# Another order of the steps of four engines between the long convolution and the second feed-forward block, with unread products ahead of 17 waits of TensorE

## What is computed

```
K  = 2 Re(sum over 64 modes of Ct exp(dtA l))           a convolution kernel for each of 256 channels
y  = irfft(rfft(x) * rfft(K)) + D x                     a convolution along 1024 tokens
x1 = layernorm(x + (layernorm(x + y) * w + b))
x2 = layernorm(x1 + attention(x1, ctx) Wo + bo)         16 heads of 16, 77 keys
s  = top 8 of (8 best row keys + 8 best column keys), for each of 4 heads
e  = sum over heads and k of silu(x2 . down[idx]) softmax(s) up[idx]
out = layernorm(x2 + (silu(x2 Wg + bg) (x2 Wu + bu)) Wd + bd + e)
```

## Time and profile before

| | |
|---|---|
| median of 3 runs | 652.65 us (652.47 to 652.74) |
| the profiled execution | 650.57 us |
| its span, first to last instruction | 648.8 us |
| TensorE busy / weight loads | 587.8 us (91%) / 383.0 us |
| VectorE busy | 493.2 us (76%) |
| ScalarE busy | 397.8 us (61%) |
| GpSimd busy | 310.8 us (48%) |
| mean granted clock of TensorE | 0.961 |

### The profile page before, as it was taken

The page is one execution under the profiler, slowest core; times in us unless marked ns, Lnnn a source line. Parts: engine busy times, 40 slices in busy tenths (PEclk is TensorE's granted clock), DMA queues, the critical chain, the costliest instruction groups (busy, mean ns, idle before and its releaser), DMA issues.

```text
span 648.8 us, 9695 instructions
## 1 busy us (share of the span) xinstructions
PE 587.8 (91%) x3186; PEld 383.0 (59%) x3186; DVE 493.2 (76%) x966; ACT 397.8 (61%) x554; POOL 310.8 (48%) x346
## 2 busy tenths in 40 slices
PE   5569799988976899999999999999999999998996
PEld 2246576766645554547867455785755587543585
DVE  7999985565688779977677897677688886778872
ACT  4777573304344579777638887754788754777750
POOL 0737586684334564333555423356443262744441
PEclk9679999979977899999999999999999999999998
DMA  8591327782700000000000000000000000000000
GB/s 240 196 367 72 107 75 199 174 165 23 317 0 1 2 2 1 0 1 2 1 8 9 10 9 0 2 0 10 9 9 9 1 2 1 17 9 8 1 17 17
DMA packets 19819, 33.88 MB, mean 52 GB/s; under 512 B 7248, under 2 KB 14161, under 8 KB 18321
## 3 DMA queue, kind: packets, MB, share of 16 engines
q1 hardware_dynamic: 15393, 29.06, 14.4%
q10 hardware_dynamic: 4376, 4.20, 2.3%
HBM read 21.55 MB, written 10.26 MB: 49 GB/s over the span
## 4 chain that ended last, share of the span: by engine, by line
PE 65%; DVE 19%; ACT 6%; POOL 3%; issue 3%; DMA 2%; DVEq 0%; POOLq 0%; SPq 0%; ACTq 0%
PE banks L838 22%; PE banks L930 8%; PE banks L935 8%; PE banks L885 4%; PE banks L907 3%; PE banks L862 3%; PE banks L897 3%; DVE stats L1481 2%; PE banks L871 2%; PE banks L922 2%; PE banks L711 2%; DVE arena L1445 2%; DVE arena L1569 1%; PE banks L768 1%; DMA arena<-scr_x 1%
## 5 line engine op out<-in xcount | busy, mean ns | idle before, releaser
L1277 POOL TENSOR_TENSOR arena<-arena 128x1024 f32<-128x1024 f32 x64 | 126.3, 1973 | 155.8 <-ACT arena L1150 154.7
L838 PE MATMUL banks<-arena 128*128 128x512 f32 x384 | 174.2, 596 | 5.7 <-issue 3.6
L838 PEld LDWEIGHTS banks<-arena 128*128 128x128 f32 x384 | 69.9, 190 | 83.1 <-issue 77.2
L1150 ACT ACTIVATE arena<-arena 128x1024 f32<-128x1024 f32 x64 | 73.5, 1149 | 7.5 <-DVE arena L1567 3.2
L1152 ACT ACTIVATE arena<-arena 128x1024 f32<-128x1024 f32 x64 | 73.5, 1149 | 2.1
L1569 DVE SCALAR_TENSOR_TENSOR arena<-arena 128x1024 f32<-128x1024 f32 x48 | 65.1, 1357 | 1.7
L1248 POOL TENSOR_SCALAR arena<-mv 128x1 f32<-128x1 f32 (+1 forms) x40 | 14.4, 361 | 100.6 <-DVE mv L1482 99.2
L930 PE MATMUL banks<-arena 128*128 128x256 f32 x256 | 58.4, 381 | 2.7 <-DVE arena L1591 1.3
L1040 ACT COPY arena<-banks 128x512 f32<-128x512 f32 (+1 forms) x64 | 34.1, 533 | 43.3 <-PE banks L830 31.2
L935 PE MATMUL banks<-arena 128*128 128x256 f32 x256 | 57.9, 379 | 0.0
L1054 ACT ACTIVATE tok<-tok,arena,rstd 128x256 f32<-128x256 f32 x48 | 27.9, 598 | 45.8 <-POOL arena L1253 44.9
(11 more groups left out here) (183 smaller groups left out, 1076.7 us busy)
## 6 DMA issues: line engine op xcount, KB each, us to landing
scr_x<-arena SPq DMA_DIRECT2D x16, 256.0 KB, 2.5
arena<-scr_x SPq DMA_DIRECT2D x2, 2048.0 KB, 11.2
scr_z<-arena ACTq DMA_DIRECT2D x13, 256.0 KB, 3.9
tok<-in_x SPq DMA_DIRECT2D x8, 256.0 KB, 5.3
arena<-scr_z SPq DMA_DIRECT2D x4, 512.0 KB
out<-tok SPq DMA_DIRECT2D x16, 128.0 KB, 1.7
arena<-scr_z SPq DMA_DIRECT2D x2, 640.0 KB
arena<-in_imat SPq DMA_DIRECT2D x1, 1152.0 KB, 5.3
```

The lines of the kernel that those rows point to most:

```text
L838: ins = mm(bk[:, :], w[:, k, P * m:P * m + P], src[:, k, :], start=(k == 0), stop=(k == KC - 1))
L1150: fn(ebuf[m % 2], sxb[m % 2], ACT.Prelu, bias=negt[:, n % 2, h:h + 1], alpha=FAR).then_inc(s_ranked, 1)
L1277: tt(sxb[m % 2], sim[:, n % 2, h, 0:XR].unsqueeze(2).broadcast_to((P, XR, NKEYS)), sim[:, n % 2, FH + h, :].unsqueeze(1).broadcast_to((P, ...
```

## The change

Three things. A table `MOVED` gives, for each engine, a new place in time to some steps; all others keep theirs. Counted as the fewest steps that have to be taken out and put elsewhere, 50 of TensorE's steps change their place, 72 of ScalarE's, 47 of VectorE's and 23 of GpSimd's, all ahead of inner.1.0 on TensorE (tile 10); behind it the lists are the same. The three groups of unread products become 17, each at the head of a step and ahead of its waits (apart from those for its bank): 38 products in place of 11, with the sixteen behind the convolution kept. And `rconv` of the last two steps lies elsewhere in the arena.

The diff, cut to its core:

```diff
+MOVED = {
+    "pe": {('conv', 7): -1.14, ('score', 0, 0): -0.75, ('score', 1, 0): -0.18, ('probs', 1, 0): 0.81,
...
+        ('score', 5, 0): 4.18, ('sim', 1): 4.2, ('score', 5, 1): 4.22, ('expert', 0, 3): 4.42,
...
+    "act": {('norm1', 0): -1.32, ('conv', 7): -0.06, ('score', 1, 1): 0.65, ('probs', 1, 0): 0.7342,
...
+    "dve": {('ln', 2): -1.14, ('ln', 3): -1.02, ('ln', 4): -0.89, ('residual', 2): -0.76, ('ln', 5): -0.46,
...
+    "pool": {('values', 0): -0.8, ('dev0', 2): -0.96, ('dev1', 2): 2.3, ('dev1', 3): 2.46, ('dev2', 0): 2.63,
...
-WARM = ((-0.5, 4, ("probs", 0, 0)), (-0.1, 5, ("probs", 0, 0)), (0.6, 2, ("turno", 0)))
+WARM = {('turn1', 0, 0): 1, ('turn1', 0, 1): 5, ('query', 0, 0): 1, ('score', 0, 0): 1, ('score', 0, 1): 1,
+        ('score', 1, 0): 3, ('probs', 1, 0): 4, ('score', 2, 1): 3, ('project', 1): 1, ('score', 3, 1): 5,
+        ('turno', 2): 5, ('probs', 3, 0): 1, ('project', 3): 1, ('sim', 0): 1, ('expert', 0, 0): 1,
+        ('probs', 4, 0): 1, ('probs', 4, 2): 3}
...
-    for at, count, before in WARM:
-        steps.append((at, ("warm", count, before)))
...
-    return [y for _, y in sorted(steps, key=lambda v: v[0] + LAG.get((engine, v[1][0]), 0.0))]
+    moved = MOVED[engine]
+    return [y for _, y in sorted(steps, key=lambda v: moved.get(v[1], v[0] + LAG.get((engine, v[1][0]), 0.0)))]
...
-        rconv = part("rconv", o_w + 4096, TILES, D)
+        rconv_of = [part(f"rconv{h}", at, B, D) for h, at in enumerate(
+            [o_w + 4096 + B * D * q for q in range(NQ - 2)] + [o_ext, o_ext + B * D])]
...
-            def warm(count, bk):
+            def idle(count, columns, start=True):
 
                 for _ in range(count):
-                    mm(bk[:, 0:D], ident[:, :], wq[:, 0, :], start=True, stop=True)
+                    mm(columns, ident[:, :], wq[:, 0, 0:columns.shape[-1]], start=start, stop=True,
+                       skip_group_check=True)
+
+            def idle_turn(step):
+
+                if step in WARM:
+                    later = PLAN[PLAN.index(step):]
+                    idle(WARM[step], t_unit(next(y for y in later if y in T_AT))[:, 0:D])
+
+            def idle_wide(step):
+
+                if step in WARM:
+                    idle(WARM[step], w_unit(step + ("a",))[:, 0:D])
...
                 elif kind == "probs":
                     j = step[2]
+                    idle_turn(step)
                     pe.wait_ge(s_exp, 2 * n + 2)
...
                 elif kind == "project":
+                    idle(WARM.get(step, 0), bank[4][:, 0:D])
                     pe.wait_ge(s_tev, T_AT[("turno", n)] + 1)
```

More of the change, by code:

```diff
@@ L818, in conv @@
                         conv_half(ahead, 0)
-                    warm(WARM_CONV, bank[4])
+                    idle(WARM_CONV, bank[4][:, 0:D])
                     pe.wait_ge(s_zr[1], 16 * (len(z_batches()) - 2 + 3))
@@ L880, in _ @@
                         if c % 4 == 0:
+                            idle(WARM.get(step + (c // 4,), 0), bank[4][:, 2 * P + 16:4 * P], start=False)
                             pe.wait_ge(s_tev, T_AT[("probs", n, c // 4)] + 1)
```

56 lines of the change are left out of this document (51 added, 5 removed), and 3 rows, old and new, of the table MOVED.

## The result

The changed kernel takes 658.22 us, the median of 8 executions (656.57 to 661.27), the kernel before in the same session 652.69 (8 executions, 650.44 to 658.34). The ratio is 1.0078, with a 95% interval of 1.005 to 1.0106: **0.8% slower, where 1.1% faster was forecast**. The profiled execution of the changed kernel took 660.39 us (span 658.6), that of before 650.57 (span 648.8).

The account below looks back on a forecast made before the run. VectorE was taken as the bound ahead of expert.0.0, TensorE behind it. 11.0 - 5.15 + 1.7 - 0.5 = 7.05, so 7 us less: 645.6 us from 652.65, range 640.8 to 649.8.

Parts of the forecast that it names:

- 11.0 us of lead: Up to expert.0.0: shorter waits on VectorE's chain let it start at 218.55 in place of 229.54.
- the cover of the five products ahead of score.3.1: Ahead of score.3.1 on TensorE: five unread products, 2.3 us, fit in a wait of 2.6 and cost nothing.
- the 0.5 us put against the moves whose lengths were not followed: Tiles 5 to 9: new waits among the other moved steps cost 0.5 us, bounds none and 1.7 us.
- the first score's wait: VectorE ahead of score.0.0: its idle 8.91 us shrink to a wait of 0.65 us.
- probs.4.2: Behind 218.5: TensorE waits 0.95 us for its bank, then three products take 1.35, together 2.3 us.
- The clock, 1.00 throughout: TensorE ahead of expert.0.0: 87% busy, against 85% in a stretch that kept 1.00, so full clock throughout.
- Given back behind 218.5, 5.15 us: Where TensorE is the bound: new waits at probs.4.0, score.5.1 and probs.4.2 cost 5.15 us together.
- The wait at score.5.1: Behind sim.1: TensorE waits 2.0 us while best.0 takes 5.8; were best.0 some 3.8, no wait, 9 us gained.
- probs.4.0: Behind 218.5: TensorE waits 0.85 us for the exponential of score.4.1, its one product inside that wait.
- The two gaps that close, 1.7 us: TensorE's gaps at turno.4 (0.76 us) and expert.1.0 (0.94) close, 1.7 us gained.
- Rival 4: Unread products stand uncovered on the path, deciding at some 60% uncovered: 4.7 us more, 657 us; chance 0.05.
- All three signs: expert.0.0 later than 223, clock below 0.9 between 186 and 218, or TensorE gaps over 2 us between tiles 5 and 9.

Follow-up runs that it names:

- The ladder: The medians of the kernels that ran, in rows that mostly differ by one named change; together some 9 us of gain and 15 us of loss.
- the kernel with the free bank: The changed kernel with the five products ahead of score.3.1 written to unread columns of bank 4 instead of a transpose bank: 652.46 us, ratio 1.0003.
- the mended kernel: Kernel before plus early moves (to expert.0.0) and their products, those at score.3.1 in free bank-4 columns, norm1.7 moved to 4.09: 643.44 us, ratio 0.986.
- the mended kernel with the moves from place 7.9 on: The mended kernel with the late moves of place 7.9 and later (tiles 8 and 9) added, norm1.7 excepted: 646.96 us, ratio 0.9918.
- the pair of runs with and without the products: The mended kernel, 643.44 us, and the same with `WARM = {}` (convolution's sixteen products kept), 652.03 us.
- The late part: The moved steps with places from 3.95 on (tiles 4 to 9); put alone into the kernel before, with its products: 665.11 us, ratio 1.0182.
- the order without products: The changed kernel with none of its 38 unread products, the sixteen behind the convolution kept: 660.33 us, ratio 1.0107.
- the early part alone: Only the moves ahead of the first feed-forward block, with all products but the three at probs.4.2, later steps as before: 652.47 us, ratio 1.0002.
- the kernel without that group: The changed kernel without the five unread products ahead of score.3.1, nothing else: 655.23 us, ratio 1.0042.

## Why the prediction was wrong, step by step

Forecast were 11.0 us of lead, 3.95 us given back behind it (5.15 - 1.7 + 0.5) and nothing for the products: 7 us less. The ladder has 9.1 us of lead, 9.0 given back and 5.8 for one group of products: 5.7 us more, beside 5.5 measured. Two terms failed. One is the cover of the five products ahead of score.3.1, costed at nothing; the other is the 0.5 us put against the moves whose lengths were not followed.

**The lead, 11.0 us: nearly right as a walk, wrong in one cover.** The parts that I followed came as written: the first score's wait (1.05 us after 8.91; I had said 0.65), and in the kernel with the free bank expert.0.0 62.0 us after turn1.0.0 where I had 60.1, so a lead of 9.0 us. (The walk was short by the other 2 us: project.3 came at 215.40 in the mended kernel, where I had 213.3.) The step that failed is "five before score.3.1 (2.3 in 2.6)", costed at nothing. I asked how long TensorE would wait for the score's own semaphore and whether the products fit in. I did not ask what the **products** wait for, though the change puts each group ahead of its step's waits "apart from those for its bank". For probs.4.2, which waits in the same way for a bank, I did see it. The wait for the bank ends at 200.30, 1.4 us after the wait it was to fill (198.88), and costs 5.8 us of the kernel, as the run with the free bank shows.

**The clock, 1.00 throughout: right but for that place.** It was 1.00 up to 186 us, 0.89 to 218, and 1.00 there too once the five products ran in time. One trace speaks against a full cure: in the mended kernel with the moves from place 7.9 on, TensorE's list and its waits from turn1.0.0 to 198 us are those of the mended kernel, but the five products of turno.2 took 4.09 us for 2.40 and the clock from 186 to 218 was 0.95.

```profile
198.43 4.09 PE L811 MATMUL banks<-wqo,ident 128*128 128x256 f32 x10
```

The Trainium skill, TensorE: Matmul & The Clock Gate, "What's actually happening", has the throttled state as the default that activity releases; the pair of runs with and without the products (1.00 and 0.80) agrees. My weighing of 87% busy against 85% was no argument for it: in the changed kernel the stretch from 186 to 229.5 is 84% busy and has 0.92, because of the one piece of it that ran at half the clock behind one idle time.

**Given back behind 218.5, 5.15 us: some 3.1 us of it came.** The wait at score.5.1 was to be 2.0 us and was 0.36, because best.0 took 4.3 us and not 5.8 (229.16 to 233.46; this was the other end that I had kept). At probs.4.2 I had 0.95 and 1.35: it was 1.03 and 1.56. At probs.4.0 I had 0.85: it was 0.19.

**The two gaps that close, 1.7 us: they did not.** turno.4 waits 0.69 us where it waited 0.76, and sim.4 with expert.1.0 together 1.11 where it was 0.49 and 0.94.

**"0.5 against it for the moves of tiles 5 to 9": the worst-sized term.** The late part costs 9.0 us by the ladder, where 5.15 - 1.7 + 0.5 made it 3.95. With 3.1 us for the waits that I followed and nothing for the gaps, some 6 us are left for this term, where I had 0.5. What I had not followed is in it: the waits at sim.2 of 1.17 us, at 284.41 of 0.65, at 286.12 of 0.44, at 366.33 of 0.62, and the 2.8 us behind inner.1.0. My bounds for it were "none, and the 1.7 us themselves": I took it that these moves could lose no more than they might win, and no row said so. Moved steps whose lengths are not followed need a bound from the trace on both sides; TensorE was busy 113.1 of 115.5 us there, so they could win 2.4 us at most in that stretch, and what they could lose had no such bound.

**Rival 4, slower at 657 us, chance 0.05,** gave nearly the right time for half of the reason; that its number came so close is luck. It named the products on the path, with 60% of them uncovered as the point where it decides. One group of 17 was on the path, and by its bank. The other half, the late part, stood in no rival. All three signs that I had named for "wrong" appeared: expert.0.0 at 229.78, later than 223 even without the 3.9 us ahead of turn1.0.0, a clock of 0.89 between 186 and 218, and over 2 us of gaps between tiles 5 and 9.

**The time before, unchanged by the edit, is not that steady.** In the profiled execution after the change the last 52 records of the convolution take 14.45 us; in the mended kernel they take 11.49. Of the nine traces with the early moves five have 11.49 and four have 13.18 to 14.45; the four traces with the old order there have it fast (44 of the records in 9.69 to 9.76). Two of the nine:

```profile
146.99 11.49 PE L832 MATMUL banks<-arena 128*128 128x256 f32 x52 [1.17 <-DMA arena<-scr_z]
```

(the mended kernel) and

```profile
145.89 13.18 PE L870 MATMUL banks<-arena 128*128 128x256 f32 x52 [2.27 <-DMA arena<-scr_z]
```

(the order without products). The 3.9 us ahead of turn1.0.0 are this: 3.0 of clock (14.45 less 11.49) and 0.7 of a later transfer (the first of the records starts at 147.70, before at 146.97). TensorE's list is the same in all kernels up to these records, so I put them down to the execution and not to the change; that is argued, not shown. It fits that one profile was 9.8 us above the other and the medians only 5.5.

**What stays open.** Which of the moves in tiles 4 to 7 costs what of the 5.5 us, and which of those from place 7.9 on what of the 3.5. The parts can't be taken out one by one: the orders of the four engines hang together there. It was taken apart no further than by place and by GpSimd's four steps. VectorE's longer pieces and TensorE's waits for VectorE go together in the traces, but that the first makes the second is argued, not shown.

## What to carry to other kernels

Work that is put into a wait has waits of its own: ask what it needs (a bank, a buffer), who gives that back, and whether that engine is itself held by the very thing that the wait is for. Test a reordering in halves: here one half was worth 9 us and the other cost 9, and together with one badly placed filler they read as a small loss that no single line of the profile explains. Where the bounding engine is as busy as here behind 229.5 us (98%), a new order can win 2% at most, and here it lost more.

## What the runs showed of the hardware

**TensorE often pays twice when it stands still for a few us.** After 4.39 idle us the ten records took 4.64 in place of 2.32, in the early part alone after 4.38 idle us 3.94. After the 3.07 idle us of the kernel without that group, attend took 3.71 for 2.42. At the convolution, after 3.30 idle us behind a transfer, 52 records took 14.45 us for 11.49; after 1.17 idle us, in the mended kernel's execution, they took 11.49. Whether it happens differs between executions: after 3.27 idle us the early part alone had 11.49 too, and the 4.09 us for ten records shown above came without an idle time of over 0.7 us in the 10 us before.

**A small piece of VectorE can last as long as the piece of GpSimd beside it.** After the change, VectorE and then GpSimd:

```profile
233.27 0.19 DVE L1629 TENSOR_TENSOR arena<-arena 128x32 f32<-128x32 f32 x1
...
245.18 1.91 DVE L1626 TENSOR_SCALAR arena<-arena 128x4 f32<-128x4 f32 x1
...
247.19 1.90 DVE L1629 TENSOR_TENSOR arena<-arena 128x32 f32<-128x32 f32 x1
```

```profile
234.64 1.90 POOL L1352 TENSOR_TENSOR arena<-arena 128x1024 f32<-128x1024 f32 x1 [1.50 <-ACT arena L1225]
...
245.17 1.90 POOL L1352 TENSOR_TENSOR arena<-arena 128x1024 f32<-128x1024 f32 x1
247.15 1.90 POOL L1338 TENSOR_SCALAR arena<-arena 128x2048 f32<-128x2048 f32 x1
```

The subtraction takes 0.19 us in GpSimd's idle 1.50 and 1.90 us where GpSimd begins a piece of 1.90 just ahead of it; a piece of four elements takes 1.91 beside another. Both end when GpSimd's does. The Trainium skill, SBUF — State Buffer, "Who interferes with whom", says that a VectorE instruction with two SBUF inputs contends with a GpSimd instruction that reads SBUF, and that issue order and not the shape of the operation decides who blocks; the rows of the subtraction agree. Which of the two got there first decides 1.7 us, and that is what made best.0 take 4.3 us and not the 5.8 that I took over from the earlier trace rows: there the piece was the one of 1.90 us, here that of 0.19.
